# Four-layer graph network on one core: the second layer's weights and half of its transposed input prepared inside the first layer's block

## The chip, the core and the metric

The kernel runs on 1 core of one Trainium2 chip. The metric is device time in microseconds of one execution; lower is better. All times below are of that one core.

## What is computed

Four graph layers follow one another, each added to its input and layer-normalised over the 64 channels. `x` is (8, 1024, 64), `adj` is (1024, 1024), both float32. The change touches the end of the first layer and the start of the second:

```python
# first layer: three adjacency powers, weights that depend on the node
w = einsum('nd,dkio->nkio', embedding, weight)
x_g = einsum('knm,bmc->bnkc', [I, A, 2*A@A - I], x)
x = layernorm(x + einsum('bnki,nkio->bno', x_g, w) + embedding @ bias)
# second layer: for each of 8 heads
h = x @ W
s = where(h @ h.T * graph == 0, -1e16, h @ h.T * graph)
heads = softmax(s) @ h + b
# then leaky_relu over the heads, the same once more with W_out, residual, layernorm
```

Two further layers follow; the change leaves them as they are.

## The kernel before

Every engine has its own instruction stream, written out by hand, and waits on semaphores. A layer (or half a layer) is a block: all engines finish one before any starts the next. The order of work on an engine is the order in which it is written.

**First layer (lines 165 to 450).** SP loads the adjacency and the eight batches of x (L284, L287), ACT the node weights (L321 to L325). TensorE transposes the adjacency (L416), multiplies it with x for eight tiles of 128 nodes (`ax` stage, L426) and, later, with the result once more (`pe_square`, L236). Then 64 tokens (a tile of nodes of one batch, numbered n; tile n // 8, batch n % 8) are worked through in 16 quads u of four. For a quad, `pe_quad` transposes the features of four tokens into the `turn` banks (L226), ACT copies them out twice (`gH`, `gW`, L336, L339) and POOL subtracts the rounded from the exact copy (`gL`, L303), so that two matmuls in the rounded type carry the full precision. `pe_products` makes ten matmuls of 512 columns for one token (L255) into one of two `zps` buffers; VectorE weighs the result (L264) and reduces it (L271). After every 16 tokens two tiles are complete, and their layer norm is spread over VectorE (L103 to L119), POOL (L134) and ACT (L138, L142), a few tokens later: group c covers tiles 2c and 2c+1 of all batches. Groups 0 to 2 are normalised while products go on, group 3 after the last token. The last `pe_square` stands in quad 11.

**Second layer, hidden part (lines 616 to 965).** The block begins with a preparation and then runs `bodies`: 32 items (4 couples of batches times 8 heads) of 16 steps each, in a hardware loop. The preparation, line by line: SP loads `wh` twice (both halves of the partitions), `wo` and `bh` (L890 to L892); TensorE transposes the eight head weights (L945), VectorE copies them (`whT`, L918), TensorE multiplies each with itself (L949, the matrix M = W W^T), VectorE splits M into a rounded part and a rest (`Mh`, `Ml`, L924, L928). For each of 8 batches TensorE transposes the 8 tiles of x (L957), ACT copies them rounded to `SX` (L909), VectorE writes the rest into the other half of the partitions (L932). POOL stages one head's M (`stage_m`, L847, L848). The product of M with `SX` in two halves gives Y (L684, L685), which ACT and VectorE split again (L912, L937). Only then does the first score matmul start (L504). POOL clears the accumulator `h2T` with one memset at the block's start (L896).

```python
pe.wait_ge(loaded, 16 * 4)                 # L943
for b in range(B):                          # L953
    if b >= 2:
        pe.wait_ge(sx_lo, b - 1)
    ...
pe.wait_ge(sx_lo, B)                        # L959
pe.wait_ge(staged_m, 1)
```

Score banks: `score_ps` are two buffers of 1024 columns, and the transposes of batch b use buffer b % 2.

## Time and profile before

| | us |
|---|---|
| median of 3 runs | 3417.58 (3417.16 to 3417.95) |
| the profiled execution's own time | 3417.75 |
| its span, first to last instruction | 3415.7 |
| TensorE busy | 3089.7 (90%) |
| VectorE busy | 2989.7 (88%) |
| ScalarE busy | 2293.5 (67%) |
| POOL busy | 820.3 (24%) |

The span is read against the profiled execution's own time: 2.05 us lie outside it. A row of the timeline gives the start, the duration, engine, line, operation, output <- inputs, the count of instructions merged into the row, and in brackets the idle time before and what ended it. Matmuls overlap, so a row's duration is longer than the time from one start to the next.

### The profile page before, as it was taken

Reading aid. Unit: us, or ns where it says so; the run is one execution under the profiler, and the core shown is the slowest. Engines: PE = TensorE matmul, PEld = TensorE weight load, DVE = VectorE, ACT = ScalarE, POOL = GpSimd, SP = SyncE. Lnnn points to the kernel's source line nnn. Section 1 sums busy time; section 2 is a strip of 40 time slices with the busy share of each in tenths; the row PEclk is TensorE's granted clock in tenths of the full one; section 3 lists DMA queues with packets and bytes.
Section 4 is the critical chain, followed back from the end, with each engine's and each line's share of the span. In section 5 each row is a group of like instructions: output and inputs, shape, how many; then the busy total and the mean of one; then the engine's idle time right before and its main releaser. Section 6 shows DMA issues by size and latency. Waiting matters only on the chain. (4 is left out here: it accounts for less than half of the span.)

```text
span 3415.7 us, 48269 instructions
## 1 busy us (share of the span) xinstructions
PE 3089.7 (90%) x15547; PEld 1884.4 (55%) x15547; DVE 2989.7 (88%) x3847; ACT 2293.5 (67%) x3481; POOL 820.3 (24%) x572
## 2 busy tenths in 40 slices
PE   7997799999999999999999999799596888888857
PEld 3665566666666666566666666599553333333323
DVE  2477899999999999999999999688738999999944
ACT  0121677777777777777777777677335999999831
POOL 0222000000000000000000000000105999999921
PEclk9998999999999999999999999899798999999978
DMA  3000000000000000000000000000000000000001
GB/s 87 1 1 10 1 1 0 0 0 0 0 0 0 0 0 0 0 0 0 0 0 0 0 0 0 1 1 0 2 7 1 1 1 1 1 1 1 0 2 25
DMA packets 30363, 12.15 MB, mean 4 GB/s; under 512 B 27984, under 2 KB 29264, under 8 KB 30288
## 3 DMA queue, kind: packets, MB, share of 16 engines
q1 hardware_dynamic: 25056, 10.04, 1.3%
q10 hardware_dynamic: 5232, 1.12, 0.2%
q8 instruction: 46, 0.75, 0.1%
q14 instruction: 29, 0.24, 0.0%
HBM read 9.06 MB, written 2.10 MB: 3 GB/s over the span
## 5 line engine op out<-in xcount | busy, mean ns | idle before, releaser
L572 ACT ACTIVATE hid_work<-hid_work,hid_nmax 128x1024 f32<-128x1024 f32 x512 | 589.1, 1151 | 305.0 <-DVE hid_nmax L556 305.0
L544 DVE TENSOR_TENSOR hid_work<-hid_score_ps,A 128x1024 f32<-128x1024 f32 x512 | 619.8, 1211 | 28.4 <-PE hid_score_ps L505 28.4
L556 DVE CUSTOM_DVE_ANT_0 hid_work<-hid_masks,hid_work 128x1024 f32<-128x1024 f32 x512 | 622.0, 1215 | 0.2 <-DVE hid_masks L564 0.2
L1591 POOL TENSOR_TENSOR el<-el,node_edge 128x1024 f32<-128x1024 f32 x256 | 611.2, 2388 | 18.4 <-DVE el L1573 12.7
L583 ACT COPY hid_probsT<-hid_turn_ps 128x512 f32<-128x512 f32 x1024 | 542.5, 580 | 98.7 <-PE hid_turn_ps L519 98.7
L519 PEld LDWEIGHTS hid_turn_ps<-ident,hid_work 128*128 128x128 f32 x4096 | 457.6, 140 | 248.0 <-issue 204.5
L519 PE MATMUL hid_turn_ps<-ident,hid_work 128*128 128x128 f32 x4096 | 544.7, 276 | 5.2 <-ACT hid_probsT L583 3.9
L745 PE MATMUL hid_mix_ps<-hid_probsT,x_now 128*64 128x512 f32 x2048 | 495.9, 604 | 34.0 <-DVE hid_Zn L819 31.1
L504 PE MATMUL hid_score_ps<-hid_SX,hid_Y 128*128 (+1 forms) x1024 | 476.5, 465 | 1.6 <-DVE hid_Yl L937 1.4
L505 PE MATMUL hid_score_ps<-hid_SX,hid_Yl 128*128 (+1 forms) x1024 | 403.3, 394 | 0.0
L1544 PE MATMUL spread<-hT_parts,pick 128*128 128x512 f32 x1024 | 307.5, 423 | 65.2 <-DVE u_buf L1567 62.1
L564 DVE TENSOR_SCALAR hid_masks<-hid_work 128x1024 f32<-128x1024 f32 x512 | 352.1, 688 | 0.0
L1567 DVE SCALAR_TENSOR_TENSOR u_buf<-spread,agg,node_edge 128x1024 f32<-128x1024 f32 x256 | 326.4, 1275 | 1.2 <-PE spread L1544 1.2
L1573 DVE SCALAR_TENSOR_TENSOR el<-ex_ps,el 128x1024 f32<-128x1024 f32 x256 | 313.5, 1225 | 2.3 <-ACT ex_ps L1606 2.3
L1602 ACT ACTIVATE el<-u_buf,agg 128x1024 f32<-128x1024 f32 x256 | 295.1, 1153 | 30.3 <-DVE u_buf L1567 10.8
L1544 PEld LDWEIGHTS spread<-hT_parts,pick 128*128 128x128 f32 x1024 | 174.0, 189 | 246.8 <-DVE u_buf L1567 216.1
L1606 ACT ACTIVATE ex_ps<-u_buf,agg 128x1024 f32<-128x1024 f32 x256 | 286.4, 1119 | 16.6 <-DVE el L1573 0.2
L861 POOL COPY x_now<-X 128x512 f32 (+1 forms) x65 | 39.9, 614 | 1047.9 <-PE hid_mix_ps L745 1047.9
L745 PEld LDWEIGHTS hid_mix_ps<-hid_probsT,x_now 128*64 128x64 f32 x2048 | 127.1, 136 | 271.4 <-issue 271.4
L1557 PE MATMUL summed<-el,wi 128*64 128x512 f32 x1024 | 252.8, 615 | 18.0 <-POOL el L1591 4.3
L504 PEld LDWEIGHTS hid_score_ps<-hid_SX,hid_Y 128*128 128x128 f32 x1024 | 193.4, 189 | 111.2 <-issue 54.6
L505 PEld LDWEIGHTS hid_score_ps<-hid_SX,hid_Yl 128*128 128x128 f32 x1024 | 193.9, 189 | 58.2 <-issue 29.9
(270 smaller groups left out, 4066.7 us busy)
## 6 DMA issues: line engine op xcount, KB each, us to landing
A<-in_adj_dram SPq DMA_DIRECT2D x4, 1024.0 KB, 9.7
X<-in_x_dram SPq DMA_DIRECT2D x8, 256.0 KB, 8.6
out_dram<-X SPq DMA_DIRECT2D x8, 256.0 KB, 3.4
wa<-in_L_gnn_weight_dram ACTq DMA_DIRECT2D x2, 256.0 KB, 14.0
wb<-in_L_gnn_weight_dram ACTq DMA_DIRECT2D x2, 256.0 KB, 14.2
wh<-in_L_gnn_Wh_dram SPq DMA_DIRECT2D x2, 256.0 KB, 4.3
incid<-in_L_gnn_H_dram SPq DMA_DIRECT2D x2, 256.0 KB, 3.5
wo<-in_L_gnn_W_out_dram SPq DMA_DIRECT2D x1, 256.0 KB, 5.0
```

What stands on the lines that cost most here:

```text
L504: nc.tensor.matmul(o, Y2[:, u, rows], move, start=True, stop=False)
L505: last_mm = nc.tensor.matmul(o, Yl[:, u, rows], move, start=False, stop=True)
L519: last_mm = nc.tensor.transpose(turn_ps[half][:, a * P:(a + 1) * P], work[:, kk % 4, b * P:(b + 1) * P], ident[:])
L544: nc.vector.tensor_tensor(work[:, kk % 4, :], score_ps[kk % 2][:], A[:, kk % NT, :], ALU.mult).then_inc(s["weighted"], 1)
L556: nc.vector.tensor_tensor_reduce(work[:, kk % 4, :], masks[:, kk % 2, :], work[:, kk % 4, :], -1.0, 3.0e38, ALU.add, ALU.min, nmax[:, kk % ...
L564: nc.vector.tensor_scalar(masks[:, kk % 2, :], work[:, kk % 4, :], 0.0, MASKED, ALU.is_equal, ALU.mult).then_inc(s["zeroed"], 1)
L572: nc.scalar.activation(work[:, kk % 4, :], work[:, kk % 4, :], ACT.Exp, bias=nmax[:, kk % 4:kk % 4 + 1], scale=-1.0, accum_out=rowsum[:, k ...
L583: nc.scalar.copy(probsT[:, kk // group % 2, half * 4:half * 4 + 4, kk % group, :], turn_ps[half][:].rearrange("p (a b) -> p a b", b=P)).th ...
L745: done = nc.tensor.matmul(mix_ps[rows, :], x_now[:, u, mt, :], at.probsT[:, half, mt].rearrange("p t q -> p (t q)"), start=(mt < 2), stop= ...
L1544: last = nc.tensor.matmul(spread[q % 2][:, cols], pick[:, f].rearrange("p h e -> p (h e)"), hT_parts[:, part, j, cols], start=(part == 0), ...
L1567: nc.vector.scalar_tensor_tensor(out=u_buf[:, q % 2, :], in0=spread[q % 2][:], scalar=agg[:, j, f:f + 1], in1=gate[:, j, :], op0=ALU.subtr ...
L1591: nc.gpsimd.tensor_tensor(el[:, q % ELS, :], el[:, q % ELS, :], coefT[:, q // C, :], ALU.mult).then_inc(s_weighted, 1)
```

## The change

- The four loads of `wh`, `wo` and `bh` are issued by SP in the first layer's block, behind those of x.
- The eight transposes of the head weights stand in front of tile 4 of the `ax` stage on TensorE, the eight products for M in front of tile 6; VectorE makes `whT`, `Mh` and `Ml` behind its copies of tiles 4 and 6. They use the `turn` banks, which are idle there.
- Tiles 0 to 3 of the normalised x (groups 0 and 1) are transposed in quads 12 to 15: two batches for each quad, four transposes behind the products k = 1 and k = 3, into the `ax` banks. ACT copies each twice (rounded into `SX`, exact into `xT_now`), and POOL, not VectorE, subtracts.
- In the second block only tiles 4 to 7 remain: half a bank for each batch, so that the two score buffers hold four batches at once. The two halves of Y are made as soon as batch 0 is there, between the transposes of batches 3, 4 and 5. `stage_m` and `stage_x` come first on POOL, the memset of `h2T` behind them.
- To find room, the buffer of the transposed adjacency shares its place with `SX`, and `R`, `w01`, `w2`, `embT`, `whT` and `xT_now` lie in other buffers (`h2T`, `zE`, `a2d`, `wa`, `wb`). TensorE waits for `m_split` before the first quad.

```diff
+        acc_scope = keep.enter_context(ExitStack())
+        h2T = sb("h2T", [P, J, N], F32, acc_scope)
+        hid_scope = keep.enter_context(ExitStack())
+        with ExitStack() as first_use:
+            AT = sb("AT0", [P, NT, N], F32, first_use)
+        SX_hid = sb("hid_SX", [P, B, N], F32R, hid_scope)
...
+            w01, w2 = zE[:, 0], zE[:, 1]
+            whT = wa[:].rearrange("p (h r) c -> p h r c", r=2)
+            xT_now = wb[0:C].rearrange("p d o -> p (d o)").rearrange("p (k n) -> p k n", k=2)
+            embT = a2d[0:D, 1].rearrange("d b r c -> d (b r c)")
+            R = h2T[:].rearrange("p j (r c) -> p (j r) c", c=C)
...
+            def early_x(u):
+
+                return range(2 * (u - 12), 2 * (u - 12) + 2) if u >= 12 else ()
...
+                for half in range(2):
+                    sp.dma_start(wh[half * C:(half + 1) * C], L1_Wh.rearrange("h c d -> c h d")).then_inc(w_loaded, 16)
+                sp.dma_start(wo[:], L1_W_out.rearrange("(h d) c -> d h c", d=HID)).then_inc(w_loaded, 16)
+                sp.dma_start(bh[:], L1_bh.rearrange("h d -> d h"), allow_slow_non_contiguous=True).then_inc(w_loaded, 16)
+                sp.wait_ge(w_loaded, 16 * 4)
...
+                    for b in early_x(u - 1):
+                        pool.wait_ge(g_lo, 2 * (u + 1))
+                        pool.wait_ge(sx_hi, b + 1)
+                        nc.gpsimd.tensor_tensor(SX_hid[C:P, b, 0:HALF], xT_now[:, b % 2], SX_hid[0:C, b, 0:HALF],
+                                                ALU.subtract).then_inc(sx_lo, 1)
+                    if early_x(u - 1):
+                        pool.wait_ge(sx_lo, 2 * (u - 12))
...
+                pool.wait_ge(norm.centred, J - 1)
+                for b in early_x(QUADS - 1):
+                    pool.wait_ge(sx_hi, b + 1)
...
+                pool.wait_ge(sx_lo, B)
...
+                    for b in early_x(u):
+                        act.wait_ge(sx_banked, b + 1)
+                        if b >= 2:
+                            act.wait_ge(sx_lo, b - 1)
+                        nc.scalar.copy(SX_hid[0:C, b, 0:HALF], ax[b % 2][0:C, :])
+                        nc.scalar.copy(xT_now[:, b % 2], ax[b % 2][0:C, :]).then_inc(sx_hi, 1)
...
+                    if t == 4:
+                        vec.wait_ge(w_turned, 1)
+                        nc.vector.tensor_copy(whT, turn[0][:].rearrange("p (h c) -> p h c", c=C).unsqueeze(2)
+                                              .to_broadcast([P, HEADS, 2, C])).then_inc(w_copied, 1)
+                    if t == 6:
+                        vec.wait_ge(m_made, 1)
...
+                    if t == 4:
+                        pe.wait_ge(w_loaded, 16 * 4)
+                        for h in range(HEADS):
+                            done = nc.tensor.transpose(turn[0][:, h * C:(h + 1) * C], wh[0:C, h, :], ident[0:C, 0:C])
+                        done.then_inc(w_turned, 1)
+                    if t == 6:
+                        pe.wait_ge(w_copied, 1)
+                        for h in range(HEADS):
+                            done = nc.tensor.matmul(turn[1][:, h * C:(h + 1) * C],
...
+                pe.wait_ge(m_split, 2)
                 pe_quad(pe, 0)
...
+                        if k % 2 == 1 and u >= 12:
+                            b = early_x(u)[k // 2]
+                            if b == 0:
+                                pe.wait_ge(norm.done, 2)
+                                pe.wait_ge(a2_copied, NT)
+                            if b >= 2:
+                                pe.wait_ge(sx_hi, b - 1)
+                            for t in range(NT // 2):
+                                last = nc.tensor.transpose(ax[b % 2][0:C, t * P:(t + 1) * P], Xrows[:, row(b, t), :], ident[:])
+                            last.then_inc(sx_banked, 1)
...
+            def x_bank(b):
+
+                return at.score_ps[b // 2 % 2][0:C, b % 2 * HALF:(b % 2 + 1) * HALF]
+
...
             def _(pool):
+                stage_m(pool, bass.ds(0, 1))
+                stage_x(pool, bass.ds(0, 1), 0)
                 nc.gpsimd.memset(h2T[:], 0.0).then_inc(cleared, 1)
-                stage_x(pool, bass.ds(0, 1), 0)
-                pool.wait_ge(loaded, 16 * 4)
-                pool.wait_ge(m_split, 2)
-                stage_m(pool, bass.ds(0, 1))
                 pool_body(pool, 0, first=True)
...
+                def x_turn(b):
+                    if b >= 4:
+                        pe.wait_ge(sx_lo, B + b - 3)
+                    for t in range(NT // 2):
+                        done = nc.tensor.transpose(x_bank(b)[:, t * P:(t + 1) * P], Xrows[:, row(b, NT // 2 + t), :], ident[:])
+                    done.then_inc(sx_banked, 1)
+
+                for b in range(4):
+                    x_turn(b)
+                pe.wait_ge(sx_lo, B + 1)
+                pe.wait_ge(staged_m, 1)
+                y_product(0, slice(0, 1)).then_inc(misc_made, 1)
+                x_turn(4)
+                pe.wait_ge(misc_read, 1)
+                y_product(1, slice(0, 1)).then_inc(misc_made, 1)
+                for b in range(5, B):
+                    x_turn(b)
+                pe.wait_ge(sx_lo, 2 * B)
                 bodies(pe, pe_step, ITEMS)
```

In the second block ACT makes the hi copies of batches 0, 1, 2, then Y half 0, batch 3, Y half 1, batch 4, then batches 5, 6, 7; VectorE follows in the same order with the rests.

**TensorE in the `ax` stage of the changed kernel** (line numbers are those of the changed kernel: L497 is the `ax` matmul, L485 a transpose of a head weight, L490 a product for M, whose operand `whT` lies in `wa`):

```order
L497 MATMUL l_ax<-X,AT 128x512 x7
L485 MATMUL l_turn<-ident,wh 128x64 [waits hid_w_loaded]
L485 MATMUL l_turn<-ident,wh 128x64 x7
L497 MATMUL l_ax<-X,AT 128x512 [waits l0_vec_copied]
L497 MATMUL l_ax<-X,AT 128x512 x7
L497 MATMUL l_ax<-X,AT 128x512 [waits l0_vec_copied]
L497 MATMUL l_ax<-X,AT 128x512 x7
L490 MATMUL l_turn<-wa 128x64 [waits hid_w_copied]
L490 MATMUL l_turn<-wa 128x64 x7
L497 MATMUL l_ax<-X,AT 128x512 [waits l0_vec_copied]
```

Before, only `ax` matmuls stand there; the 16 short ones stood at the head of the second block.

**POOL from quad 12 to the end of the first block, changed kernel** (L328 is the subtraction for `gL`, L333 and L350 the new ones for `SX`, L341 adds the bias, L134 centres a norm group):

```order
L328 TENSOR_TENSOR gL<-gW,gH 128x512 [waits l0_z_summed,l0_g_copied] x8
L333 TENSOR_TENSOR hid_SX<-wb,hid_SX 64x512 [waits hid_sx_hi,l0_g_lo] x2
L341 TENSOR_TENSOR X<-X,Eb 128x4x128 [waits hid_sx_lo]
L341 TENSOR_TENSOR X<-X,Eb 128x4x128
L134 TENSOR_TENSOR h2T<-h2T,norm_stats 128x4x256 [waits norm_meaned]
L328 TENSOR_TENSOR gL<-gW,gH 128x512 [waits l0_z_summed,l0_g_copied] x2
L333 TENSOR_TENSOR hid_SX<-wb,hid_SX 64x512 [waits hid_sx_hi,l0_g_lo] x2
L328 TENSOR_TENSOR gL<-gW,gH 128x512 [waits l0_z_summed,l0_g_copied,hid_sx_lo]
```

Eight subtractions came in; the bias and the centring of group 2 now stand behind the first two of them, and the `gL` of quads 14 and 15 behind two and four.

**TensorE at the head of the second block, changed kernel** (L1006 transposes a tile of x, L750 and L751 make Y, L585 is the first score matmul):

```order
L1006 MATMUL hid_score_ps0<-ident,X 64x128 x8
L1006 MATMUL hid_score_ps1<-ident,X 64x128 x8
L750 MATMUL hid_misc_ps<-hid_SX,mh_now 128x512 [waits hid_staged_m,hid_sx_lo]
L751 MATMUL hid_misc_ps<-hid_SX,ml_now 128x512
L1006 MATMUL hid_score_ps0<-ident,X 64x128 [waits hid_sx_lo]
L1006 MATMUL hid_score_ps0<-ident,X 64x128 x3
L750 MATMUL hid_misc_ps<-hid_SX,mh_now 128x512 [waits hid_misc_read]
```

Behind it come L751, three more groups of four transposes (batches 5, 6 and 7) and L585. Before, 16 matmuls on the head weights, 64 transposes and then both halves of Y stood in front of the first score; now there are 32 transposes, with Y among them.

## Rows read from the trace of the kernel before

**Rows 1.** The page's first line.
```profile
span 3415.7 us, 48269 instructions
```
**Rows 2.** Busy time of each engine by stage, granted clock as PEclk.
```profile
core 0: us, PE busy (x) PEld busy (x) DVE busy (x) ACT busy (x) POOL busy (x), PEclk, DMA share, GB/s
...
27.00:88.50 61.50, 59.23 (x160) 27.44 (x159) 18.64 (x20) 2.34 (x4) 0.00 (x0) 1.00 0.03 5
...
333.50:367.10 33.60, 16.40 (x92) 12.64 (x92) 14.93 (x15) 9.95 (x11) 5.15 (x5) 0.70 0.15 24
367.10:2164.80 1797.70, 1753.34 (x9472) 1084.95 (x9472) 1754.63 (x2624) 1356.83 (x2433) 75.38 (x223) 1.00 0.00 0
```
**Rows 3.** Timeline, end of the first block and head of the second.
```profile
332.02 1.23 DVE L119 TENSOR_TENSOR X<-R,norm_stats 128x1024 f32<-128x1024 f32 x1
333.54 1.36 SPq L890 DMA_DIRECT2D wh<-in_L_gnn_Wh_dram  x2
333.54 3.51 POOL L896 MEMSET h2T<- 128x4096 f32 x1 [4.64 <-POOLq L165]
...
340.40 1.11 PE L945 MATMUL hid_turn_ps<-ident,wh 64*128 64x64 f32 x8 [21.95 <-DMA bh<-in_L_gnn_bh_dram]
```
**Rows 4.** Timeline, the same preparation, M products and transposes of x.
```profile
342.83 3.67 PE L949 MATMUL hid_turn_ps<-whT 128*128 128x64 f32 x16 [1.32 <-DVE whT L918]
346.29 3.49 PE L957 MATMUL hid_score_ps<-ident,X 128*64 128x128 f32 x16
...
350.55 1.06 PE L957 MATMUL hid_score_ps<-ident,X 128*64 128x128 f32 x8 [0.77 <-DVE hid_SX L932]
```
**Rows 5.** Timeline, the second half of Y and the loop's start.
```profile
364.50 0.80 PE L684 MATMUL hid_misc_ps<-hid_SX,mh_now 128*128 128x512 f32 x1 [1.40 <-DVE hid_Yl L937]
...
367.12 0.79 PE L504 MATMUL hid_score_ps<-hid_SX,hid_Y 128*128 128x512 f32 x1 [1.40 <-DVE hid_Yl L937]
...
369.31 1.23 DVE L544 TENSOR_TENSOR hid_work<-hid_score_ps,A 128x1024 f32<-128x1024 f32 x1 [2.24 <-PE hid_score_ps L505]
```
**Rows 6.** Timeline, 16 short matmuls at the full clock, in the block after the hidden part.
```profile
2216.88 1.90 PE L533 MATMUL fin_mix_ps<-V,fin_probsT 128*128 128x64 f32 x16
```
**Rows 7.** Timeline, VectorE, weighing two tokens in a row.
```profile
298.72 1.23 DVE L264 TENSOR_TENSOR zE<-l_z,emb 128x1024 f32<-128x1024 f32 x1
...
301.18 1.23 DVE L264 TENSOR_TENSOR zE<-l_z,emb 128x1024 f32<-128x1024 f32 x1
```
**Rows 8.** Timeline, TensorE: four transposes of quad 14; first and last product of token 63.
```profile
285.75 0.60 PE L226 MATMUL l_turn<-ident,XA 128*128 128x128 f32 x4
...
315.87 0.50 PE L255 MATMUL l_z<-w_hi,gH 128*128 128x512 f32 x1
...
318.06 0.39 PE L255 MATMUL l_z<-w_both,gL 128*128 128x512 f32 x1
```
**Rows 9.** Timeline, VectorE, a norm step with two SBUF inputs, and the last token.
```profile
283.86 1.22 DVE L103 TENSOR_TENSOR R<-R,X 128x1024 f32<-128x1024 f32 x1
...
320.72 1.23 DVE L264 TENSOR_TENSOR zE<-l_z,emb 128x1024 f32<-128x1024 f32 x1
```
**Rows 10.** Groups by line, 0 to 334 us: POOL's subtraction for gL.
```profile
L303 POOL TENSOR_TENSOR gL<-gW,gH 128x512 fp32r<-128x512 f32 x32 | 40.7, 1292 | 232.1 <-ACT gW L339 232.1
```
**Rows 11.** Busy time in short stretches: first loads, a clock drop, the loop's start.
```profile
29.00:30.00 1.00, 0.85 (x8) 0.85 (x8) 0.25 (x2) 0.43 (x1) 0.00 (x0) 1.00 0.00 0
...
92.80:101.70 8.90, 8.87 (x17) 3.55 (x16) 0.69 (x1) 0.00 (x0) 0.00 (x0) 0.81 0.00 0
...
368.00:370.00 2.00, 2.00 (x6) 1.52 (x6) 0.69 (x1) 0.00 (x0) 0.00 (x0) 0.50 0.00 0
370.00:374.00 4.00, 3.39 (x13) 1.83 (x11) 3.97 (x6) 0.43 (x1) 0.00 (x0) 1.00 0.00 0
```
**Rows 12.** Timeline, the same `pe_square` of 8 matmuls, with and without a clock drop.
```profile
92.84 8.83 PE L236 MATMUL l_ax<-XA,AT 128*128 128x512 f32 x16
...
103.77 7.03 PE L236 MATMUL l_ax<-XA,AT 128*128 128x512 f32 x16
```

More of the change, by code:

```diff
@@ L470, in bodies, with attention @@
                 step(engine, count, k, last=True)
-        def attention(scope, tag, group):
+        def attention(scope, tag, group, SX):
             s = {}
@@ L937, in _ @@
                     nc.vector.tensor_tensor(Yl[:, 0, cols], misc_ps[:], Y2[:, 0, cols], ALU.subtract).then_inc(misc_read, 1)
+                    x_lo(3 + half)
+                for b in range(5, B):
+                    x_lo(b)
                 vec.wait_ge(cleared, 1)
```

116 lines of the change are left out of this document (45 added, 71 removed).

## Prediction

> **What bounds the kernel now.** I read the profile from the whole to the place. The page gives the span, 3415.7 us [rows 1]. The busy times by stage come next [rows 2]: in the hidden part's loop TensorE is busy 1753.34 and VectorE 1754.63 of 1797.70 us, and the change edits nothing in it, so no time can come from there. The stretch in front of it, 333.50 to 367.10, is 33.60 us long, and no engine is busy for half of it: it is a chain of waits. The `ax` stage, 27.00 to 88.50, is the opposite: TensorE 59.23 of 61.50 us. What TensorE gets to do there lengthens the kernel.
>
> The timeline shows the chain's links. The first block ends when VectorE has normalised the last group, 332.02 + 1.23 = 333.25; 0.29 us later POOL and SP start the second [rows 3]. TensorE starts at 340.40, having waited for the load of `bh` [rows 3]: 6.9 us of loads. The head weights (transposes, copy, products, split) take until the transposes of x start at 346.29 [rows 4]: 5.9 us. Then 64 transposes, eight copies and eight subtractions that hand two buffers round, until the first half of Y, and both halves of Y in turn; the loop's first score matmul starts at 367.12 [rows 5].
>
> **The second block after the change.** The start is 333.5 before; I count from there. Loads and head weights are gone. What remains:
> - 16 transposes for batches 0 to 3 without a wait between them: the first 16 of before took 3.49 us at the clock that TensorE has there [rows 4]. TensorE is then free for Y half 0 at 3.4. Batch 0's rest is ready earlier (its four transposes end at 0.9; a copy of 0.6 and a subtraction of 0.7 follow), and so is `stage_m`.
> - From the start of one half of Y to the start of what waits for it took 367.12 - 364.50 = 2.62 us [rows 5]: matmuls, ACT's copy, VectorE's subtraction. Two halves in turn: 3.4 + 5.2 = 8.6.
> - Behind Y half 1 VectorE still has the rests of batches 4 to 7. A half bank is 512 columns; four of them at about 0.6 us are 2.4, if their transposes are ready: 11.0. The transposes of batches 5 to 7 start only when Y half 1 has left TensorE, at about 7.1, and at 0.87 us each (3.49 / 4) end at 9.8; a copy, the last subtraction and their hand-overs bring 11.3.
>
> I take 11.3, so the gain is 33.6 - 11.3 = **22.3 us**. The bounds: 10.4 if the full clock returns halfway (eight transposes took 1.06 us there, four half of that [rows 4]), 13.5 if the two chains on ACT and VectorE hinder each other by one copy and one subtraction for each half of Y. The memset is behind `stage_m` and `stage_x` now: about 1.2 + 3.51 us [rows 3], done by 4.8, and VectorE asks for it at 11. Without that cover it would cost what is missing. From the first score to VectorE's first product took 2.19 us before, partly at the half clock [rows 5, 11]; I leave it as it is.
>
> **What the first block pays.** The loads stand behind x on SP's queue. By 29 us nothing moves on the DMA engines any more [rows 11], x is asked for at about 33, and the weights are asked for at tile 4, about 61: they took 6.9 us from issue to the last landing. SP has nothing else there. Price: nothing.
> - The M products are 16 records of a 128-row operand against 64 columns. The same shape took 1.90 us at the full clock [rows 6] and 3.67 at the half clock [rows 4]; in a chain 0.2 of it overlaps: 1.75, as the granted clock in the stage is 1.00 [rows 2]. The eight transposes of head weights took 1.11 at the half clock [rows 3]; half of that is 0.6. Both lie on the path: **+2.4 us**, with the bounds 2.1 and 4.6 (both at the half clock).
> - VectorE has one copy of 0.69 us in each 6.9 us of that stage and takes `whT` (1.2) and the split (2.6) into the gaps. TensorE asks for `whT` a tile later, for the split at the first quad. Nothing. `R`, `w01` and the rest only change place: nothing.
> - Quads 12 to 15. Here VectorE is what binds: it weighs a token each 301.18 - 298.72 = 2.46 us [rows 7], TensorE needs 2.3 and is at the end of token 63's products at 318.45, while VectorE takes them up at 320.72 [rows 8, 9]: 2.3 us in hand. 16 tokens (36.8), two quads' transposes (1.8) and eight new groups of four transposes are TensorE's work; a group of four is 0.44 us from start to start (four took 0.60 with its end [rows 8]), 3.5 in all. VectorE's own work in that stretch is 16 x 2.46 and 5.4 of norm. Laid side by side, token by token, with two `zps` buffers, TensorE stays ahead except at token 56, which slips by 0.2 to 0.3. The last group stands behind the last product. **+0.3 us**; the bounds are 0 and 3.5 (nothing hidden).
> - Who waits behind the new waits? ACT's copies of a batch wait for TensorE's transposes late in a quad, and behind them stand the Square and Sqrt of group 2: Square moves from 288.6 to about 299, and VectorE asks at 303; Sqrt to 310.4, asked for at 317. On POOL eight subtractions come in, of 1.29 us if 64 rows cost what 128 do [rows 10]; `gL` of quad 14 moves from 288.5 to 293.4, and TensorE needs both by 298.3; quad 15's from 299.3 to 301.3, needed by 308.6. So 2.3 us of cover at the narrowest place. Without it every late microsecond would be one of the span.
> - The tail: batches 6 and 7 are subtracted on POOL by about 322, centring of group 3 is due at 327. Nothing.
>
> **Against the trace.** L103 adds two SBUF buffers on VectorE in 1.22 us, with POOL idle beside it [rows 9]; VectorE's time is the path there. The new POOL subtractions read SBUF, and by the count above the first would end at 284.0, within 0.2 us of where L103 of group 2 starts; the one for batch 6 ends 0.5 before L119. If the two engines got in each other's way, a VectorE step could wait for a POOL step, 1.29 us, twice: +2.6. No row of before shows such a pair overlapping, so the sum takes 0 and the case is a rival. The Trainium skill, "SBUF — State Buffer", section "Who interferes with whom", says that a VectorE instruction with two SBUF inputs and a GpSimd one that reads SBUF exclude each other for a whole instruction; by that rule the sum is 0 to 2.6 higher, without it as above.
>
> **Clock.** After a light stretch at 88 to 93 us the mean granted clock of the next 8.9 us was 0.81 [rows 11]: 3.4 of them at the half level, 1.2 GHz. The `pe_square` there took 8.83 us, the next one 7.03 [rows 12]. The stretch comes 2.4 us later now, so the drop can be missing or come twice: 1.8 us either way, here and likewise at later drops. The sum takes 0.
>
> **Sum.** -22.3 + 2.4 + 0.3 = -19.6. The profiled execution took 3417.75, 0.17 above the median 3417.58; 3417.75 - 19.6 = 3398.1, and by the median 3398.0. I say **3398.0**. A measurement of this kernel can tell about 0.2%, 6.8 us, from no change.
>
> **Rivals.**
> 1. *The four engines' new hand-overs in quads 12 to 15 don't fit the gaps.* All eight groups of transposes exposed (3.5 instead of 0.3), or a `gL` late by as much: 3401.2. For it: four engines wait for each other, with 2.3 us at the narrowest place. Against: TensorE's own surplus. With the half clock in the `ax` stage (+2.2) it is 3403.4.
> 2. *POOL and VectorE exclude each other* (the rule above): 3398.0 + 1.3 or + 2.6 = 3399.3 to 3400.6.
> 3. *The clock comes back inside the shorter preparation and the drop at 93 stays away*: -0.9 -1.8, and 0.9 more by faster first scores: 3394.4.
> 4. *The change doesn't do what it says:* the freed time becomes another wait in front of the loop, on the memset, on the last copies, or on code that an engine starts cold. If the loop starts 20 us behind the block's start, 3406.7. Against: 0.29 us from VectorE's end to the others' start, and the memset's 3.51 [rows 3].
> 5. *Slower: the half clock goes into the loop.* Place: the first steps of `bodies`. The new preparation has only scattered TensorE work after an idle tail of 15 us. Before, the clock was still halved at 368 to 370 and full at 370 to 374 [rows 11]. At the half level TensorE would need twice its time; the loop takes 1797.7 / 32 = 56 us an item and TensorE is busy 98% of it, so each item at half clock costs about 55 us more. It decides from 20 / 55 of an item, 6 steps; two thirds of an item would give 3398 + 37 = 3435. Against: the full clock came back within 4 us of the first score before.
>
> **How the numbers follow.** Forecast 0.62 (3395.5 to 3400.5), rival 1 0.12, rival 2 0.09, rival 3 0.10, rival 4 0.05, rival 5 0.02. 8 in 10 need the forecast and the nearer parts of rivals 1 to 3: 3393.5 to 3403.0; the bounds of the priced terms lie within, save when several err the same way. All but parts of rivals 4 and 5 are more than 6.8 us faster: faster 0.97, same 0.02, slower 0.01.
>
> **What would show it.** Right: block start to first score about 11.3 us; VectorE's end of the first block 2.7 later, at about 336; the `ax` stage longer by 2.4, and quads 12 to 15 by less than 1; L103 and L119 still at 1.2. Wrong: a first score later than 13.5 us after the block's start (rival 4), TensorE waiting for `gL` in quads 14 and 15 (rival 1), a VectorE step of 2.5 us beside a POOL one (rival 2), a granted clock of 0.50 past the third step (rival 5).

## The result and the profile after

The changed kernel takes **3401.9 us** (median of 5 runs, 3399.56 to 3402.88); the kernel before, run beside it, 3417.58 (3417.16 to 3419.93). The ratio is 0.9952, with an interval of 0.994 to 0.9965. The gain is 15.7 us where 19.6 was forecast; 3401.9 lies inside the range of 3393.5 to 3403.0, near its slow end, and outside the narrower band of the forecast itself (3395.5 to 3400.5).

The page's first lines of the changed kernel, for [rows 1]: TensorE's busy time is what it was (3089.7 before), so the 15.3 us by which the span fell were waiting.
```profile
span 3400.4 us, 48309 instructions
## 1 busy us (share of the span) xinstructions
PE 3089.6 (91%) x15547; PEld 1884.6 (55%) x15547; DVE 2984.8 (88%) x3847; ACT 2295.9 (68%) x3497; POOL 830.8 (24%) x580
```
Busy time by stage, for [rows 2]: the `ax` stage, the head of the second block, the hidden part's loop. The head is 10.5 us instead of 33.6, and VectorE is now busy for 6.59 of it.
```profile
core 0: us, PE busy (x) PEld busy (x) DVE busy (x) ACT busy (x) POOL busy (x), PEclk, DMA share, GB/s
28.00:91.50 63.50, 61.54 (x183) 29.81 (x182) 22.20 (x25) 2.34 (x4) 0.00 (x0) 1.00 0.11 17
337.90:348.40 10.50, 6.96 (x37) 5.36 (x37) 6.59 (x10) 6.59 (x11) 5.07 (x5) 0.79 0.00 0
348.40:2147.50 1799.10, 1755.80 (x9472) 1086.09 (x9472) 1754.32 (x2624) 1354.27 (x2432) 75.38 (x223) 1.00 0.00 0
```
To see where the 15.3 us come from I cut both executions at the same instructions and took the start of each from the timeline. The pieces add up to the difference of the spans:

| piece, from and to | before | after | difference | forecast |
|---|---|---|---|---|
| start to the first `ax` matmul | 33.56 | 34.58 | +1.02 | 0 |
| `ax` stage, to the copy of `embT` | 56.09 | 58.70 | +2.61 | +2.4 |
| to VectorE's first weighed token (two `pe_square`) | 24.38 | 24.38 | 0 | 0 +-1.8 |
| tokens and norm, to the end of the first block | 219.22 | 219.91 | +0.69 | +0.3 |
| block's end to the next block's start | 0.29 | 0.31 | +0.02 | 0 |
| block's start to the first score matmul | 33.58 | 10.51 | -23.07 | -22.3 |
| first score to VectorE's first product | 2.19 | 1.62 | -0.57 | 0 |
| from there through the loop's first item | 67.09 | 68.72 | +1.63 | 0 |
| rest of the loop, and the blocks behind it up to the last | 2809.17 | 2809.98 | +0.81 | 0 |
| last block (the fourth layer's second half) | 170.14 | 171.72 | +1.58 | 0 |

What the change itself does comes to -23.07 - 0.57 + 2.61 + 0.69 = -20.3, close to the forecast -19.6. (The 0.57 is in part a matter of where the clock stood at the first scores: over the kernels with the change that piece is 1.30 to 1.62 us, and 2.18 with the head weights alone.) The other 5 us are in places that the change does not edit.

**The head of the second block**, timeline of the changed kernel, for [rows 3 to 5]. The 16 transposes, Y's halves 2.60 us apart, and VectorE's last four subtractions stand where the prediction put them. The 12 last transposes took 1.47 us, at the full clock (the half clock had been assumed for them), and VectorE was ready for its last four subtractions 2.08 us after the second half of Y began (345.83 against 343.75), where the working charged 2.62 once more.
```profile
336.35 1.22 DVE L119 TENSOR_TENSOR X<-h2T,norm_stats 128x1024 f32<-128x1024 f32 x1
...
337.88 0.29 POOL L913 CAST mh_now<-Mh 128x128 fp32r<-128x128 f32 x1 [4.65 <-SPq L693]
...
337.90 3.60 PE L1006 MATMUL hid_score_ps<-ident,X 128*64 128x128 f32 x16 [14.57 <-PEq L179]
341.15 0.78 PE L750 MATMUL hid_misc_ps<-hid_SX,mh_now 128*128 128x512 f32 x1
...
343.75 0.50 PE L750 MATMUL hid_misc_ps<-hid_SX,mh_now 128*128 128x512 f32 x1 [0.94 <-DVE hid_Yl L993]
...
344.32 1.47 PE L1006 MATMUL hid_score_ps<-ident,X 128*64 128x128 f32 x12
...
345.86 2.48 DVE L986 TENSOR_TENSOR hid_SX<-hid_score_ps,hid_SX 64x512 fp32r<-64x512 f32 x4
...
348.39 0.50 PE L585 MATMUL hid_score_ps<-hid_SX,hid_Y 128*128 128x512 f32 x1 [2.60 <-DVE hid_SX L986]
...
350.01 1.23 DVE L625 TENSOR_TENSOR hid_work<-hid_score_ps,A 128x1024 f32<-128x1024 f32 x1 [1.68 <-PE hid_score_ps L586]
```
**The `ax` stage**, timeline, for [rows 6] and the 1.11 us of [rows 3]: the transposes of the head weights and the products for M, with the durations that were forecast for the full clock.
```profile
62.21 0.71 PE L485 MATMUL l_turn<-ident,wh 64*128 64x64 f32 x8
...
76.69 1.90 PE L490 MATMUL l_turn<-wa 128*128 128x64 f32 x16
```
**Quads 12 to 15**, timeline, for [rows 7 to 10]. L103 took 1.22 us before and takes 1.55, beside POOL's first early subtraction; and VectorE waits 0.34 us for TensorE's products at token 56. The two are 0.67 of the stage's 0.69 us.
```profile
286.75 1.28 POOL L333 TENSOR_TENSOR hid_SX<-wb,hid_SX 64x512 fp32r<-64x512 f32 x1 [2.95 <-ACT wb L399]
...
287.56 1.55 DVE L103 TENSOR_TENSOR h2T<-h2T,X 128x1024 f32<-128x1024 f32 x1
...
305.44 1.22 DVE L284 TENSOR_TENSOR zE<-l_z,emb 128x1024 f32<-128x1024 f32 x1 [0.34 <-PE l_z L275]
```
**The last block.** The 64 matmuls of the layer's wide product, timeline of before (first row) and of the changed kernel (second). Same work, same number, 1.2 us longer, and the block 1.58. TensorE had been idle for 32 us before both.
```profile
3329.48 29.34 PE L1888 MATMUL l2d_wide<-node_edge,X 128*128 128x512 f32 x64 [32.46 <-DVE X L119]
```
```profile
3312.99 30.55 PE L1945 MATMUL l2d_wide<-node_edge,X 128*128 128x512 f32 x64 [32.45 <-DVE X L119]
```
Busy time of the product's first 16 us, before and after: TensorE is busy throughout in both, at a mean granted clock of 0.90 and of 0.82. So about 3.2 us of the 16 before and 5.8 after are at the half level; behind them both are at the full one. The clock does not fall here, it comes back later.
```profile
3329.50:3345.50 16.00, 16.00 (x34) 7.15 (x35) 12.34 (x15) 1.75 (x4) 1.90 (x1) 0.90 0.00 1
```
```profile
3313.00:3329.00 16.00, 16.00 (x31) 7.08 (x32) 12.34 (x15) 1.38 (x3) 1.90 (x1) 0.82 0.01 1
```

### The profile page after: what moved, and what is told of

Same layout as the page of the kernel before. It is cut to its first block and busy times, and to the rows that moved or that the text cites. A ratio compares the mean times of both kernels' runs of the same rounds, so it can differ in the third digit from the quotient of the medians.

```text
span 3400.4 us, 48309 instructions
## 1 busy us (share of the span) xinstructions
PE 3089.6 (91%) x15547; PEld 1884.6 (55%) x15547; DVE 2984.8 (88%) x3847; ACT 2295.9 (68%) x3497; POOL 830.8 (24%) x580
## 3 DMA queue, kind: packets, MB, share of 16 engines
q10 hardware_dynamic: 5232, 1.12, 0.2%
## 5 line engine op out<-in xcount | busy, mean ns | idle before, releaser
L585 PE MATMUL hid_score_ps<-hid_SX,hid_Y 128*128 (+1 forms) x1024 | 477.3, 466 | 2.6 <-DVE hid_SX L986 2.6
L1659 ACT ACTIVATE el<-u_buf,agg 128x1024 f32<-128x1024 f32 x256 | 295.2, 1153 | 28.9 <-DVE u_buf L1624 10.4
L585 PEld LDWEIGHTS hid_score_ps<-hid_SX,hid_Y 128*128 128x128 f32 x1024 | 193.7, 189 | 111.3 <-issue 54.5
## 6 DMA issues: line engine op xcount, KB each, us to landing
wa<-in_L_gnn_weight_dram ACTq DMA_DIRECT2D x2, 256.0 KB, 14.6
```

What stands on the lines that cost most here:

```text
L585: nc.tensor.matmul(o, Y2[:, u, rows], move, start=True, stop=False)
```

## The experiments

The profiles are compared by the pieces of the table above: each experiment aims at one piece, and the total is only a cross-check, since it moves by several us with things that no experiment touches (see "both kernels once more"). The kernel before alone, run beside the experiments, took 3415.13 to 3422.43 us.

### The head weights alone

x is prepared wholly in the second block, as before the change; loads, M and its split stay early.
```diff
             def early_x(u):
-                return range(2 * (u - 12), 2 * (u - 12) + 2) if u >= 12 else ()
+                return ()
...
-                for b in range(3):
-                    x_hi(b)
+                for b in range(B):
+                    act.wait_ge(sx_banked, b + 1)
+                    nc.scalar.copy(SX[0:C, b, :], at.score_ps[b % 2][0:C, :]).then_inc(sx_hi, 1)
```


> The head weights and their products stay in the first block, the whole transposed x is prepared in the second block as before the change. My theory (the gain is the sum of three links of a chain: loads 6.9 us, head weights 5.9, early half of x with Y put in between 10.3): the second block takes 33.6 - 12.8 = 20.8 us to its first score, the first block pays 2.6, so about 3417.6 - 10.2 = 3407.4. Rival (the loads and the weights would have been hidden beside the transposes of x, which could have gone first, and the gain is that of x alone): above 3412. Second question: after the loop's start the changed kernel lost 2.1 us to the end of the hidden part and 1.6 more in the last block. If that comes from where the granted clock happens to fall (theory), this kernel shows other lumps of up to 1.7 us in other places, each with a stretch of halved clock; if it comes from the new places of the buffers (rival), it shows the same 2.1 and 1.6.

Measured: 3411.16 us, ratio 0.9977 (0.9967 to 0.9987). From the block's start at 337.32 to the first score at 357.92 it is 20.60 us; the `ax` stage is 58.71, and tokens and norm are 219.24, as before the change. Timeline:
```profile
337.34 3.59 PE L993 MATMUL hid_score_ps<-ident,X 128*64 128x128 f32 x16 [15.12 <-PEq L179]
...
353.52 0.50 PE L748 MATMUL hid_misc_ps<-hid_SX,mh_now 128*128 128x512 f32 x1 [2.35 <-DVE hid_SX L978]
...
357.92 0.79 PE L583 MATMUL hid_score_ps<-hid_SX,hid_Y 128*128 128x512 f32 x1 [1.40 <-DVE hid_Yl L983]
```
So the early weights are worth 33.58 - 20.60 = 13.0 us of the chain and cost 2.6 in front: the chain is right. The total is 4 us above what was expected of it; its profile has the same +1.6 in the loop's first item and +1.6 in the last block as the changed kernel's. On the second question that is what the rival said (the buffers' new places); it is answered further down, where profiles with the same places lack them.

L103 takes 1.22 us here, with `R` already in its new place and no early subtraction on POOL.

### The early x alone

Loads and early x stay; transposes, products and split of the head weights go back to the second block, `stage_m` behind the memset.
```diff
-                    if t == 4:
-                        pe.wait_ge(w_loaded, 16 * 4)
-                        for h in range(HEADS):
...
+                for h in range(HEADS):
+                    done = nc.tensor.transpose(at.turn_ps[0][:, h * C:(h + 1) * C], wh[0:C, h, :], ident[0:C, 0:C])
+                done.then_inc(w_turned, 1)
+                pe.wait_ge(w_copied, 1)
```


> The loads and half of x stay early, but the head weights are transposed, multiplied and split at the head of the second block. Theory: 5.9 us at the half clock come back in front of the transposes of x (16.4 from block start to first score), 2.6 are saved in the ax stage: 3401.9 + 3.3 = 3405.2. Rival (VectorE's and TensorE's work on the weights fits into the gaps of the chain): under 3403.

Measured: 3404.59 us, ratio 0.9952 (0.9936 to 0.9968). That median is over five executions of which one took 9417.91 us; the other four have 3402.8, which is the rival's "under 3403". The total cannot decide between the two; the pieces do, and they say what the theory said. Block's start (336.27) to first score (352.57): 16.30 us; `ax` stage 56.08, as before the change; tokens and norm 219.86. The 5.9 us from the first row below to the last are what M costs at the head of a block, at the half clock:
```profile
336.29 1.09 PE L997 MATMUL hid_turn_ps<-ident,wh 64*128 64x64 f32 x8 [14.58 <-PEq L179]
...
338.70 3.67 PE L1001 MATMUL hid_turn_ps<-whT 128*128 128x64 f32 x16 [1.32 <-DVE whT L963]
342.16 3.22 PE L993 MATMUL hid_score_ps<-ident,X 128*64 128x128 f32 x16
```
Early M buys 16.30 - 10.51 = 5.8 us and costs 2.6. Early x costs the quads 0.56 to 0.69 us in every kernel that has it and leaves POOL's order as it is, and nothing in the one that doesn't have it (219.24 against 219.22 before).

### The products for M twice

```diff
+                        for h in range(HEADS):
+                            done = nc.tensor.matmul(turn[1][:, h * C:(h + 1) * C],
+                                                    whT[:, h].rearrange("p r c -> p (r c)"), whT[:, h, 0, :], start=True,
+                                                    stop=True)
                         done.then_inc(m_made, 1)
```


> The eight products for M are made twice in the ax stage. Theory: TensorE binds there and every short matmul counts in full: the ax stage is 1.7 to 1.8 us longer, the run 3401.9 + 1.8 = 3403.7 (give or take one lump of 1.7 where the clock falls). Rival (the 2.6 us of the changed kernel are mostly the switch between kinds of matmul, not their work): under 0.5 longer.

Measured: 3402.36 us, ratio 0.9949 (0.9933 to 0.9966); the `ax` stage is 60.50 us, 1.80 more than the changed kernel's 58.70. Timeline, both sets:
```profile
75.82 1.89 PE L490 MATMUL l_turn<-wa 128*128 128x64 f32 x16
77.55 1.95 PE L494 MATMUL l_turn<-wa 128*128 128x64 f32 x16
```
The whole second set lies on the path: nothing hides TensorE's work in this stage.

### Both kernels once more

> The kernel before, profiled a second time. The first profile's last block took 170.1 us from its first load to the end, four profiles of the changed kernel and its variants 171.7, and the difference sits where the halved clock ends. Theory (where the clock's changes fall differs from run to run, whatever the kernel): this profile may show 171.7 too, or a shift elsewhere; its first ax matmul, at 33.6 in the first profile and 33.7 to 34.7 in the others, moves too. Rival (the changed kernel itself made the last block longer): 170.1 and 33.6 again.

> The changed kernel again, as the reference on this chip for the two below. 3399.5 to 3403. From the second block's start to the first score 10.5 us, the quads 0.7 longer than before, the ax stage 2.6; if the clock does not fall in the loop's first item, that item is 1.65 us shorter than in the first profile (67.05 instead of 68.7 from the first product to the second item's staging).

Measured: the kernel before 3417.55 us; the changed kernel 3398.88, ratio 0.9945 (0.9929 to 0.9962). The spans are 3415.5 and 3397.7. The changed kernel was expected at 3399.5 to 3403 and is 0.6 below that, though its first item kept the longer time (68.66). The kernel before repeats itself piece by piece, to 0.2 us: its last block is 170.17 us again, which is what the rival said (the changed kernel itself lengthens that block), not the theory. Later profiles speak against the rival: three kernels with the change have 170.12 to 170.19 there. The changed kernel does in all pieces but two: its first `ax` matmul starts at 33.81 (34.58 in the first profile), and the piece with the two `pe_square` is 22.66 us where it was 24.38. The first of the two, timelines of the first profile of the changed kernel, of this one, and of the early x alone:
```profile
96.47 8.83 PE L256 MATMUL l_ax<-XA,AT 128*128 128x512 f32 x16
```
```profile
95.71 7.13 PE L256 MATMUL l_ax<-XA,AT 128*128 128x512 f32 x16
```
```profile
94.24 9.52 PE L256 MATMUL l_ax<-XA,AT 128*128 128x512 f32 x16
```
It is one fall of the clock, none, and two in a row. One costs 1.70 us in these rows; of the two, 2.39 us are in the row and 0.93 in the matmuls just ahead of it (2.92 instead of 1.99). Over the 14 profiles of this study the piece is 22.7 us four times, 24.4 six times and 26.0 four times, and nothing between.

The moment at which the work arrives, counted from the first instruction, does not decide it. Up to this piece the changed kernel, "Y half 0 first" and "the memset first" run the same instructions. The first `ax` matmul started at 34.58 us in the changed kernel and at 34.57 with Y half 0 first, and the piece was 24.38 and 22.66. It started at 33.81 in the changed kernel's second profile and at 33.80 with the memset first, and the piece was 22.66 and 25.98.

Two other places move likewise: the loop's first item is 67.02 to 67.09 us in seven profiles and 68.66 to 68.73 in the other seven; the last block is 170.12 to 170.19 in five, 171.72 to 171.74 in eight, and 172.15 in one.

### Y half 0 first

`SX` of tiles 0 to 3 is complete when the second block starts, so the first half of Y needs nothing of it but `stage_m`. The cut shows TensorE's order; ACT's copies and VectorE's subtractions are put in the same order.
```diff
-                for b in range(4):
-                    x_turn(b)
-                pe.wait_ge(sx_lo, B + 1)
                 pe.wait_ge(staged_m, 1)
                 y_product(0, slice(0, 1)).then_inc(misc_made, 1)
-                x_turn(4)
+                for b in range(3):
+                    x_turn(b)
+                pe.wait_ge(sx_lo, B + 1)
                 pe.wait_ge(misc_read, 1)
                 y_product(1, slice(0, 1)).then_inc(misc_made, 1)
-                for b in range(5, B):
+                for b in range(3, B):
                     x_turn(b)
```


> Y half 0 needs only the half of batch 0 that the first block has made, so it goes in front of all transposes in the second block, and half 1 behind three of them. Theory (the chain there is: first transposes, Y half 0, Y half 1, four rests): the 3.4 us in front of the first Y fall to 0.6, TensorE at the half clock then needs until 4.2 for three groups, and from Y half 1 on 5.1 remain: 9.3 instead of 10.5 us, 1.2 less than the changed kernel. Rival (VectorE's ten operations and their hand-overs bind, not their order): 10 or more.

Measured: 3396.61 us, ratio 0.9945 (0.9929 to 0.9962); block's start (336.04) to first score 9.58 us, 0.93 less than 10.51. That is nearer to the theory's 9.3 than to the rival's 10, and 0.3 short of it.

> Y half 0 first, once more, on the same chip as the version with the kept clock. Block start to first score 9.6 as before, time within 3 us of the first measurement (3396.6); a profile whose first-layer clock drop (near 93 us) is there again would be 1.7 us longer than the one in which it was missing.

Measured: 3397.65 us, ratio 0.9944 (0.993 to 0.9958), the chain 9.56. These two profiles are of one kernel and differ in three places: the loop's first item has 67.02 in the first and 68.69 in the second, the last block 171.72 and 170.12, and the long piece between them 2809.20 and 2810.52. Every buffer is in the same place in both, so none of the three is due to the places alone. Busy time in short stretches there, of the first and of the second (the seventh column of numbers is the granted clock):
```profile
367.00:371.00 4.00, 4.00 (x28) 2.85 (x25) 3.69 (x7) 3.21 (x6) 0.00 (x0) 1.00 0.00 0
```
```profile
367.00:371.00 4.00, 4.00 (x18) 2.81 (x15) 2.85 (x4) 1.90 (x5) 0.00 (x0) 0.57 0.00 0
```
TensorE is busy for all of the 4 us both times, at 2.4 GHz and mostly at 1.2 GHz, 28 instructions against 18. In the two microseconds ahead it had been busy for 0.76 and 1.20.

### The full clock kept over the border of the blocks

16 matmuls whose result is unused stand behind token 63 in the first block, 3 more in front of the first score.
```diff
+                for k in range(16):
+                    nc.tensor.matmul(turn[0][:], A[:, 0, 0:P], A[:, 0, 0:HALF], start=True, stop=True)
...
+                for k in range(3):
+                    nc.tensor.matmul(at.turn_ps[0][:], A[:, 0, 0:P], A[:, 0, 0:HALF], start=True, stop=True)
                 pe.wait_ge(sx_lo, 2 * B)
```


> Adds sixteen matmuls on TensorE behind the first block's last transposes, where it was idle for 14.6 us, and three behind the last transposes of the second block; their results are used by nobody. Theory (the half clock costs the preparation): the granted clock stays at 1.00 over the border, the 16 transposes take 1.9 instead of 3.6 us, each half of Y 2.0, and the first score comes 8.4 to 8.9 us after the block's start instead of 10.5; the drop at the loop's first steps stays away, 0.5 more. 2 to 3 us less than the changed kernel. Rival (ACT's and VectorE's hand-overs bind, the clock costs nothing): within 0.5 of it. A second rival: the added matmuls end later than VectorE's last step and the block starts later.

Measured: 3400.09 us, ratio 0.9947 (0.9931 to 0.9964). The granted clock is 1.00 on both sides of the border and the 16 transposes take 1.91 us instead of 3.60; block's start (338.81) to first score is 8.79 us. Busy time by stretch, and the transposes in the timeline:
```profile
324.00:338.80 14.80, 13.99 (x35) 5.99 (x32) 10.78 (x12) 2.33 (x4) 3.16 (x2) 1.00 0.00 0
338.80:347.60 8.80, 7.70 (x43) 5.08 (x43) 6.42 (x10) 6.39 (x11) 5.09 (x5) 1.00 0.01 2
```
```profile
338.83 1.91 PE L1008 MATMUL hid_score_ps<-ident,X 128*64 128x128 f32 x16 [0.84 <-PEq L179]
```
The half clock at the block's head costs 1.72 us of the chain. None of it showed in the total, which was expected 2 to 3 us below the changed kernel's and came 1.2 above the 3398.88 of the changed kernel's second measurement, made beside it. Its profile had two falls near 95 us (26.0), one in the loop's first item, and the longest last block of all (172.15).

### POOL's early subtractions twice

The first of each two writes to an unused buffer.
```diff
+                        nc.gpsimd.tensor_tensor(spare[:, b % 2], xT_now[:, b % 2], SX_hid[0:C, b, 0:HALF],
+                                                ALU.subtract)
                         nc.gpsimd.tensor_tensor(SX_hid[C:P, b, 0:HALF], xT_now[:, b % 2], SX_hid[0:C, b, 0:HALF],
                                                 ALU.subtract).then_inc(sx_lo, 1)
```


> The changed kernel with each of POOL's eight early subtractions of x made twice (the first copy of the result goes to an unused buffer). Nothing else moves. If the prediction's count of 2.3 us of cover at POOL's narrowest place holds, two more subtractions of 1.28 us for each quad (2.6 us) eat it nearly exactly: quads 12 to 15 to the end of the block get longer by 0 to 1 us, total +0 to +1 against the changed kernel. Rival 1 (the hand-overs are already on the path): the quads get longer by 1.3 to 2.6 for each pair, 5 to 10 us in all. Rival 2 (POOL and VectorE exclude each other): a VectorE step with two SBUF inputs (the norm's L103 or L119) that falls beside a POOL step shows 2.5 instead of 1.22 us; with twice as many POOL steps such a pair must now overlap at least once.

Measured: 3401.18 us, ratio 0.9951 (0.9936 to 0.9966); tokens and norm 219.87 us, against 219.91 with single ones. (The two of quad 15, whose code stands elsewhere, stay single: six were doubled.) 7.7 us more of POOL's work cost nothing, so rival 1 falls. One of the added steps met L103. Timeline:
```profile
288.54 1.55 DVE L103 TENSOR_TENSOR h2T<-h2T,X 128x1024 f32<-128x1024 f32 x1
288.97 2.26 POOL L336 TENSOR_TENSOR hid_SX<-wb,hid_SX 64x512 fp32r<-64x512 f32 x1
```
POOL had been at the duplicate from 287.73 to 289.01. L103, due at 288.54, took 1.55 us; the POOL step behind took 2.26 where all others take 1.28 to 1.31. That is what taking turns gives: L103 waits for the first POOL step, and the second POOL step waits for L103. By the recorded ends L103 had 0.47 us of the first step left to wait for and was 0.33 longer; the second POOL step had 1.12 us of L103 left and was 0.98 longer. Both waits are 0.14 us shorter than the recorded rest; why is open.

### POOL kept apart from L103

Y half 0 first, the 16 unused matmuls of the tail but none in front of the score, and one wait:
```diff
                     for b in early_x(u - 1):
+                        if b == 0:
+                            pool.wait_ge(added, 3)
                         pool.wait_ge(g_lo, 2 * (u + 1))
```


> Three edits in places that the profile keeps apart. (1) Y half 0 first. (2) The unused matmuls only behind token 63, none in front of the first score: block start to first score 8.5 to 8.7 us, since VectorE's chain there is ten subtractions of 0.62 us from 1.96 us on; 8.9 with the trailing ones. If the clock falls again without them, 9.6. (3) POOL's first early subtraction waits until VectorE's L103 of group 2 has started and ended. In every kernel with the subtraction on POOL, L103 took 1.55 us where it takes 1.22 alone, and started 0.8 us after the POOL step did. If the two exclude each other for a whole step, L103 is back to 1.22 us and the quads' stage (218.9 to 219.9 us from the first weighed token to the end of the block) falls by 0.33 us, to 219.5. If the 0.33 us has another cause (the new place of R in another buffer), L103 stays at 1.55. Time: 3393 to 3396 us, with one or two falls of the clock of 1.7 us each more or less.

Measured: 3396.6 us, ratio 0.9937 (0.9924 to 0.9951), 0.6 above the expected 3393 to 3396. Timeline: L103 is back at 1.22 us, the POOL step starts behind it, and the gap at token 56 (0.34) is as it was.
```profile
287.33 1.22 DVE L103 TENSOR_TENSOR h2T<-h2T,X 128x1024 f32<-128x1024 f32 x1
```
```profile
288.63 1.29 POOL L335 TENSOR_TENSOR hid_SX<-wb,hid_SX 64x512 fp32r<-64x512 f32 x1 [5.06 <-DVE h2T L103]
```
Tokens and norm take 219.54 us: 0.24 less than the 219.78 of Y half 0 first, 0.37 less than the changed kernel, where 0.33 was due. The two profiles of Y half 0 first have 219.78 and 219.90, so 0.24 to 0.37 is what can be said. L103 works on the same buffers as in the changed kernel, so the new place of `R` is not the cause. Block's start (337.33) to first score (346.00) is 8.67 us.

### The memset first

```diff
+                nc.gpsimd.memset(h2T[:], 0.0).then_inc(cleared, 1)
                 stage_m(pool, bass.ds(0, 1))
                 stage_x(pool, bass.ds(0, 1), 0)
-                nc.gpsimd.memset(h2T[:], 0.0).then_inc(cleared, 1)
```


> The changed kernel with POOL's memset of the accumulator in front of stage_m and stage_x at the head of the second block, as before the change. By the prediction the memset (3.51 us) is hidden only because it stands behind them: now M is staged at 3.5 + 0.6 = 4.1 us after the block's start, while TensorE asks for it at 3.3, so block start to first score grows from 10.5 to 11.3 to 11.4. If M was not what the first half of Y waits for last, nothing changes: 10.5.

Measured: 3403.32 us, ratio 0.9956 (0.9941 to 0.9972); block's start (338.62) to first score (350.00) is 11.38 us, 0.87 more. Timeline:
```profile
338.62 3.51 POOL L959 MEMSET h2T<- 128x4096 f32 x1 [4.64 <-POOLq L179]
...
342.07 0.29 POOL L913 CAST mh_now<-Mh 128x128 fp32r<-128x128 f32 x1
...
342.75 0.77 PE L750 MATMUL hid_misc_ps<-hid_SX,mh_now 128*128 128x512 f32 x1 [0.49 <-DVE hid_SX L986]
```
The cover of the memset is real and is the order on POOL.

### Y half 0 first, with the kept clock

The edits of the two experiments together.

> Both halves of the earlier two runs together: Y half 0 before any transpose of the second block, and matmuls whose result is unused from token 63 to the end of the first block and behind the last transposes, so that TensorE's clock stays at its full level. The chain then is VectorE's: it can start at 1.7 us (Y half 0, ACT's copy) and has ten subtractions of 0.62 us, 6.2 us: block start to first score 7.9 to 8.4, against 9.6 (Y first alone) and 8.8 (full clock alone). Total 1.2 to 1.7 us below Y first alone if the clock falls at the same places in both, up to 3 us either way if it doesn't.

Measured: 3397.38 us, ratio 0.994 (0.9926 to 0.9953). Block's start (335.18) to first score (344.09) is 8.91 us, not 7.9 to 8.4. VectorE's chain starts at 1.96 us and its last subtraction ends at 8.61, so ten steps take 6.65 with their hand-overs, not 6.2; the three matmuls in front of the score, still running, cost another 0.24 (without them it was 8.67). The total is 0.3 below Y half 0 first, measured beside it (3397.65), not 1.2 to 1.7. The profile has none of the three longer times (22.66, 67.07 and 170.19 us), and its span is 3392.2, the shortest of all.

## Why the prediction was right, and by what it was off

**The number.** 3401.9 is in the range partly by luck. What the change does was forecast within 0.7 us, but only as a sum: the chain and the first product gained 1.3 us more than forecast, and the `ax` stage and the quads paid 0.6 more. The places that the sum took at nothing then added 5 us in the first profile; in the second, whose execution took 3399.55, they added 2.4.

**The second block, -22.3: right, -23.07 measured.** The links stood where the working had them: 16 transposes without a wait (3.49 forecast, 3.60), the halves of Y 2.62 apart (2.60), four subtractions behind (2.4; 2.48). The 0.8 us on top is the lower bound of that term, 10.4, which came true (10.51): the full clock was back for the second half of Y, which took 2.08 instead of 2.62, and for the last 12 transposes, so VectorE and not TensorE ended the chain. "From the first score to VectorE's first product [...] I leave it as it is" missed 0.57.

**The `ax` stage, +2.4: right, +2.61.** M's products cost 1.80 by doubling (1.75 forecast), at the granted clock of 1.00.

**Quads, +0.3: under-sized, +0.69.** The slip at token 56 was there with 0.34. The rest, 0.33, is rival 2, which the sum took at nothing: POOL's subtraction was in progress when L103 came due, and L103 waited for the rest of it. The working had put the two within 0.2 us of each other and priced a whole step (1.3); they overlapped by half a microsecond. L103 took 1.54 to 1.56 us in the ten profiles where the POOL step starts 0.8 us ahead of it, and 1.22 in the one where they are apart and in the one without early x; one POOL step that came second took 2.26. Weighing a token, with one input in PSUM (TensorE's result memory) and one in SBUF, took 1.23 us also where POOL's `gL` or its new subtraction ran beside it. The Trainium skill, "SBUF — State Buffer", section "Who interferes with whom", has it that a VectorE instruction with two SBUF inputs and a GpSimd one that reads SBUF shut each other out for a whole instruction, and that the one issued first wins; the traces agree. The Trainium skill says there too that a VectorE instruction with at most one SBUF input, outside certain fast modes, does not contend with GpSimd; the 1.23 us agree.

**Rival 1 fell**: six more POOL steps in the narrowest places cost 0.0. **Rival 4 fell**: loads, memset and last copies stayed hidden, and the memset's cover is worth 0.87 us. **Rival 5 fell**: the half clock was there at the first scores (349.0 to 352.5 us; before, up to 370), once more in the first item, which cost 1.63 us, and the mean granted clock of the whole loop was 1.00 as before. **Rival 3** came true in its first half (the full clock back within the preparation, faster first scores), and in its second in some profiles only.

**The clock, "the sum takes 0": this term was mis-sized.** It was sized at one place, 93 us, as 0 or 1.8 either way, and "likewise at later drops" was not counted. At least three places have 1.6 to 1.7 us of half clock more or less from one profile to the next: near 93 us, in the loop's first item, and at the start of the last block's wide product, where the full clock comes back earlier or later. In the first profile of the changed kernel they gave 0 + 1.63 + 1.58 = +3.2; in the second -1.7 + 1.6 + 1.6 = +1.5. The kernel with Y half 0 first and the kept clock had -1.7, 0 and 0. The kernel before has one fall at the first place and neither of the other two, both times. At the first place the arrival of the work does not decide, as the pairs above show (24.38 and 22.66 us with starts 0.01 us apart); the prediction reasoned that the stretch comes 2.4 us later and that the fall could therefore go or double. Both were seen, but also between profiles in which it came at the same moment. What decides at any of the three is open. Whether the change makes the longer times in the first item and the last block more frequent is open too: they stand in seven and in nine of the twelve profiles with parts of the change, and in none of the two without.

**What remains open.** The first `ax` matmul started at 33.35 and 33.56 us in the kernel before and at 33.7 to 34.7 in all others; whether the buffers' new places cost half a microsecond of the first loads or this is spread was not tried. +0.8 us lie in 2810 us of later stages and were not followed up; two profiles of one kernel differ by 1.3 there, so they need not be the change's.

**A version that is better in its parts** is the one with Y half 0 first, POOL kept apart and the tail's unused matmuls: 1.84 us less in the chain and 0.33 to 0.37 in the quads than the changed kernel. Its ratio, 0.9937 (0.9924 to 0.9951), overlaps those of the changed kernel (0.9952, 0.9945), so by the time alone it is not shown to be faster than that; it is faster than the kernel before.

## What to carry to other kernels

A chain of waits at a block's head can be priced link by link from the same links of the old trace, and independent preparation belongs under the neighbour's slack; here 23.6 us left the path for 3.3 put onto it. Price what TensorE gets where it binds at its full duration, and what other engines get by the next step that asks for them; look then for a pair of VectorE and POOL steps that both read two buffers in SBUF at the same moment. And where a gain is a few parts in a thousand, count every place where the clock may fall or come back late, not only the nearest: here each added or took 1.6 to 1.7 us between profiles of one and the same kernel. More than one profile of each kernel, compared piece by piece, helps to tell such steps from what the change does.

## What the runs showed of the hardware

- A fall of TensorE's clock to 1.2 GHz came while TensorE was busy all the time (367 to 371 us, mean granted clock 0.57), behind two microseconds in which it was busy for 1.20; in another profile of the same kernel it stayed away (1.00, behind 0.76). One such fall costs 1.6 to 1.7 us. With the same instructions and starts 0.01 us apart the first layer had one fall or none, and none or two.
- VectorE's add of two SBUF inputs and POOL's subtraction of two take turns: whichever comes second waits for the rest of the first (0.33 us more for VectorE with 0.47 us left of the first by the records, 0.98 more for POOL with 1.12 left).
- Behind 14.6 us of idle TensorE at a block's border the next block's first 16 transposes took 3.60 us, at a granted clock of 0.50; with TensorE kept busy through the border they took 1.91, at 1.00, and the chain was 1.72 us shorter.
